# An eight-stage hybrid network on one core: a joint value and denominator product in local attention, two norms in a row as one, input and result moved tile by tile

## The reference

```
def _layernorm(x, axis=-1, eps=1e-05):
    m = jnp.mean(x, axis=axis, keepdims=True)
    v = jnp.var(x, axis=axis, keepdims=True)
    return (x - m) / jnp.sqrt(v + eps)
def rms(x, w):
    return x * jax.lax.rsqrt(jnp.mean(x * x, axis=-1, keepdims=True) + EPS) * w
x = x + _L0_attn_a_ref(_layernorm(x, axis=-1), ...)
x = x + _L0_attn_b_ref(_layernorm(x, axis=-1), ...)
attn = jax.nn.softmax(sim, axis=-1)
out = jnp.einsum('bhwij,bhwjd->bhwid', attn, bv)
```

## Time and profile before

| | us |
|---|---|
| median of 3 runs | 6118.09 |
| the profiled execution | 6125.03 |
| its span, first to last instruction | 6123.2 |
| TensorE busy (share of the span) | 5316.8 (87%) |
| VectorE busy | 3563.9 (58%) |
| ScalarE busy | 3332.0 (54%) |
| GpSimd busy | 2568.9 (42%) |
| mean granted TensorE clock | 0.946 |

### The profile page before, as it was taken

How to read it: one execution, slowest core, us unless ns; L and a number is a source line. 1 busy time by engine, 2 the same in 40 slices (tenths; PEclk the granted TensorE clock), 3 DMA queues, 4 the chain that set the end, 5 groups by cost and what they waited for, 6 DMA issues and landing times. The chain is left out here.

```text
span 6123.2 us, 113557 instructions
## 1 busy us (share of the span) xinstructions
PE 5316.8 (87%) x39222; PEld 2810.7 (46%) x39222; DVE 3563.9 (58%) x4189; ACT 3332.0 (54%) x4968; POOL 2568.9 (42%) x1902
## 2 busy tenths in 40 slices
PE   5866888888888998999897999899897999787999
PEld 2322555555544554554343554555343444343443
DVE  4757999999964553554354554554554343554444
ACT  4745888888854553554454554455354333443343
POOL 1333999999943662663133662664231000000000
PEclk8986999999999999999898999999899999888999
DMA  1002111111110110110000110111000210001111
GB/s 43 17 10 83 31 31 32 32 30 31 31 52 24 43 43 10 42 42 19 4 15 25 42 42 14 42 41 28 28 15 20 55 41 14 0 0 28 38 33 28
DMA packets 143957, 182.98 MB, mean 30 GB/s; under 512 B 33584, under 2 KB 86960, under 8 KB 142512
## 3 DMA queue, kind: packets, MB, share of 16 engines
q1 hardware_dynamic: 143792, 180.85, 11.1%
HBM read 80.31 MB, written 12.85 MB: 15 GB/s over the span
## 5 line engine op out<-in xcount | busy, mean ns | idle before, releaser
L2502 POOL TENSOR_TENSOR arena<-arena,wbig 128x1024 f32<-128x1024 f32 x512 | 1191.4, 2472 | 107.7 <-ACT arena L2438 107.6
L2489 DVE TENSOR_TENSOR_SCAN arena<-banks,arena 128x1024 f32<-128x1024 f32 x512 | 1140.6, 2278 | 68.4 <-ACT banks L2433 49.4
L963 ACT ACTIVATE arena<-banks,wbig 128x512 f32<-128x512 f32 x512 | 351.8, 687 | 591.2 <-PE banks L921 582.5
L1020 DVE TENSOR_TENSOR arena<-arena 128x512 f32<-128x512 f32 x512 | 353.2, 692 | 470.7 <-ACT arena L963 436.4
L2433 ACT ACTIVATE banks<-banks 128x1020 f32<-128x1020 f32 x512 | 518.1, 1012 | 108.5 <-PE banks L2354 100.9
L1510 POOL TENSOR_TENSOR arena<-arena 128x512 f32<-128x512 f32 x256 | 354.9, 1386 | 527.3 <-DMA arena<-arena 527.3
L635 DVE TENSOR_REDUCE arena<-banks 128x4 f32<-128x1024 f32 (+1 forms) x384 | 401.7, 1046 | 280.0 <-PE banks L462 225.7
L2438 ACT COPY arena<-banks 128x1024 f32<-128x1024 f32 x512 | 520.8, 1017 | 51.2 <-POOL arena L2502 29.9
L571 ACT ACTIVATE Y<-banks 128x2048 f32<-128x2048 f32 x192 | 305.6, 1592 | 306.4 <-PE banks L498 236.4
L931 PE MATMUL banks<-arena,wbig 128*128 128x512 f32 x1024 | 463.5, 598 | 0.0
L921 PE MATMUL banks<-Z,wbig 128*128 x1024 | 459.1, 593 | 0.0
(11 more groups left out here) (304 smaller groups left out, 9887.0 us busy)
## 6 DMA issues: line engine op xcount, KB each, us to landing
arena<-arena SPq DMA_DIRECT2D x1024, 64.0 KB, 2.0
arena<-scratch_g SPq DMA_DIRECT2D x64, 512.0 KB, 10.8
wbig<-wbig SPq DMA_DIRECT2D x48, 240.0 KB, 3.1
wbig<-scratch_d SPq DMA_DIRECT2D x512, 16.0 KB, 1.7
wbig<-scratch_b SPq DMA_DIRECT2D x64, 128.0 KB, 2.2
wbig<-scratch_c SPq DMA_DIRECT2D x64, 128.0 KB, 2.1
arena<-Z SPq DMA_DIRECT2D x64, 128.0 KB, 2.1
wbig<-in_l_ffn SPq DMA_DIRECT2D x1, 4197.0 KB, 12.4
```

The source lines that it names most:

```text
L963: act.activation(hid[e % 2][:, f, :], hbank[f], ACT.Relu, bias=b1[:, e, f:f + 1])\
L1020: last = dve.tensor_tensor(hid[e % 2][:, f, :], hid[e % 2][:, f, :], gate[u][:, e, :], ALU.mult)
L2489: dve.tensor_tensor_scan(own, line(decay_bank[n % 2]), own, 0.0, ALU.mult, ALU.add)\
L2502: pool.tensor_tensor(four(h[par][:, m * 1024:m * 1024 + 1024]), four(us[n % 2]), Bs[par].unsqueeze(1).to_broadcast([128, 4, SEQ]), ALU.mult)\
```

## The change

It has five parts.

1. In `values` the ones move into the weights: v is laid out as [v of head 2f, ones, v of head 2f+1], 64 columns each, and each product takes 128 of these columns, so that one full-width product gives the values of a head in one half of the partitions and its denominators in the other. 16 passes on half the columns become 8 passes on all 128.
2. So the copy of v (L1349) writes with gaps, the Ln of the denominators (L1355) becomes two instructions of 64 partitions that read one half and write the other, the product L1452 becomes two of 64 partitions, and the first block fills the ones with two memsets of 128x512.
3. Two norms in a row are one. With centred x and variance v the second root is of (1+e2) v + e1 e2. `attn_b` has one norm with that root. In `l0_attn_a` one centred norm gives both results, with a second Ln and Exp on ACT and two products on DVE for each tile.
4. The constants are loaded first, then X in 8 DMAs of 256 KB each with its own semaphore; SP waits in that block for the constants alone. The first weights are issued after it. PE waits for its tile at each centring of the first norm.
5. The last norm issues a store on SP for each tile when it is done, in place of the one store after it.

The core of the diff:

```diff
@@ -120,17 +120,21 @@
...
-def copy_dram_stage(k, name, pairs):
+def load_stage(k, x, pairs):
...
     landed = [Count(k, f"landed{n}", 16) for n in range(len(pairs))]
+    tiles = [Count(k, f"x_landed{t}", 16) for t in range(TILES)]
     with k.nc.Block() as block:
...
                 sp.dma_start(dst, src).then_inc(landed[n].sem, 16)
+            for t in range(TILES):
+                cols = slice(t * TILE, (t + 1) * TILE)
+                sp.dma_start(k.X[:, cols], x[:, cols]).then_inc(tiles[t].sem, 16)
             for n in range(len(pairs)):
                 sp.wait_ge(landed[n].sem, landed[n].at(16))
-
+    return tiles
@@ -155,7 +160,8 @@
...
         pe_order += [("var", t)] + ([("center", t + ahead)] if center and t + ahead < TILES else [])
-        act_order += [("ln", t), ("exp", t)] + ([("sq", t + ahead)] if t + ahead < TILES else [])
+        act_order += [("ln", t), ("exp", t)] + ([("ln2", t), ("exp2", t)] if second is not None else [])
+        act_order += [("sq", t + ahead)] if t + ahead < TILES else []
     biased = any(b is not None for _, _, b in outs)
@@ -164,6 +170,8 @@
...
     pre = [k.arena.take(TILE) for _ in range(bufs)]
+    rs2 = [k.arena.take(TILE) for _ in range(bufs)] if second is not None else rs
+    root_last, look_last = ("exp2", "ln2") if second is not None else ("exp", "ln")
     cbank = [k.psum[:, u, :] for u in range(bufs)]
@@ -176,6 +184,8 @@
...
                 if what == "center":
+                    if landed is not None:
+                        pe.wait_ge(landed[t].sem, landed[t].at(16))
                     if t >= bufs:
@@ -183,7 +193,7 @@
...
                     if t >= bufs:
-                        pe.wait_ge(act_s.sem, act_s.at(0, f"ln{t - bufs}"))
+                        pe.wait_ge(act_s.sem, act_s.at(0, f"{look_last}{t - bufs}"))
                     pe.matmul(vbank[t % bufs], k.c["mean"], sq[t % bufs], start=True, stop=True)\
@@ -203,7 +213,14 @@
...
                         act.wait_ge(dve_s.sem, dve_s.at(0, f"z{t - bufs}"))
-                    act.activation(rs[t % bufs], vbank[t % bufs], ACT.Ln, bias=k.c[eps]).then_inc(act_s.sem, 1)
+                    act.activation(rs[t % bufs], vbank[t % bufs], ACT.Ln, bias=k.c[eps], scale=scale)\
+                        .then_inc(act_s.sem, 1)
+                elif what == "ln2":
+                    act.activation(rs2[t % bufs], vbank[t % bufs], ACT.Ln, bias=k.c[second[0]], scale=second[1])\
+                        .then_inc(act_s.sem, 1)
+                elif what == "exp2":
+                    act.wait_ge(act_s.sem, act_s.at(0, f"ln2{t}"))
+                    act.activation(rs2[t % bufs], rs2[t % bufs], ACT.Exp, scale=-0.5).then_inc(act_s.sem, 1)
                 else:
@@ -212,16 +229,17 @@
...
             for t in tiles:
-                dve.wait_ge(act_s.sem, act_s.at(0, f"exp{t}"))
+                dve.wait_ge(act_s.sem, act_s.at(0, f"{root_last}{t}"))
                 if biased and t >= bufs:
                     dve.wait_ge(dve_s.sem, dve_s.at(0, f"b{t - bufs}"))
-                for dst, w, b in outs:
+                for n, (dst, w, b) in enumerate(outs):
+                    root = rs2[t % bufs] if n else rs[t % bufs]
                     to = pre[t % bufs] if b is not None else columns(dst, t)
...
                     if w is None:
-                        last = dve.tensor_tensor(to, c, rs[t % bufs], ALU.mult)
+                        last = dve.tensor_tensor(to, c, root, ALU.mult)
                     else:
-                        last = dve.scalar_tensor_tensor(out=to, in0=c, scalar=w, in1=rs[t % bufs],
+                        last = dve.scalar_tensor_tensor(out=to, in0=c, scalar=w, in1=root,
                                                         op0=ALU.mult, op1=ALU.mult)
@@ -233,6 +251,16 @@
...
                     last.then_inc(dve_s.sem, 1)
+
+        if store is not None:
+            stored = Count(k, "stored", 16 * TILES)
+
+            @block.sync
+            def _(sp):
+                for t in tiles:
+                    sp.wait_ge(dve_s.sem, dve_s.at(0, f"b{t}"))
+                    sp.dma_start(columns(store, t), columns(outs[0][0], t)).then_inc(stored.sem, 16)
+                sp.wait_ge(stored.sem, stored.at(16 * TILES))
@@ -1044,11 +1072,12 @@
...
-def l1_ffn(k, name, w):
+def l1_ffn(k, name, w, store=None):
     norm_stage(k, f"{name}_ln", k.X, [(k.Z, None, None)], True, "eps5")
...
     mixture_stage(k, f"{name}_mix", k.Z, w, k.Y, k.H)
-    norm_stage(k, f"{name}_last", k.H, [(k.X, w["gamma"], w["beta"])], True, "eps5", add_to=k.X)
+    norm_stage(k, f"{name}_last", k.H, [(k.X, w["gamma"], w["beta"])], True, "eps5", add_to=k.X,
+               store=store)
@@ -1110,7 +1139,7 @@
...
     qkb = pairs(k.arena.take_bf16(8 * SEQ), 8)
-    v = [take(2 * 512).rearrange("p (c h d) -> p c h d", c=2, h=WHEADS) for _ in range(2)]
+    v = [take(2 * 4 * 192).rearrange("p (c f s d) -> p c f s d", c=2, f=4, s=3) for _ in range(2)]
     prob = [pairs(take(2 * 320), 2) for _ in range(2)]
@@ -1120,7 +1149,7 @@
...
     obank = [k.psum[:, 6 + n, :] for n in range(2)]
-    cleared = Count(k, "cleared", 5)
+    cleared = Count(k, "cleared", 7)
     ones = k.c["ones"]
@@ -1133,13 +1162,15 @@
...
             dve.memset(mx, 0.0).then_inc(cleared.sem, 1)
+            for par in range(2):
+                dve.memset(v[par][:, :, :, 1, :], 1.0).then_inc(cleared.sem, 1)
             for m, (scale, partner) in enumerate(((w["qs"], w["qp"]), (w["ks"], w["kp"]))):
...
                     .then_inc(cleared.sem, 1)
-            dve.wait_ge(cleared.sem, cleared.at(5))
+            dve.wait_ge(cleared.sem, cleared.at(7))
@@ -1235,12 +1266,10 @@
...
                     for r in range(2):
-                        pe.matmul(to[half_rows(r), first:first + n], v[par][:, c, 2 * f + r, :],
-                                  prob[f % 2][:, r, at:at + n], start=(c == 0), stop=True, skip_group_check=True)
-                for c, at, n, first in ((0, 0, 192, 0), (1, 192, 128, 128)):
-                    for r in range(2):
-                        last = pe.matmul(to[half_rows(r), SEQ + first:SEQ + first + n], ones[:, 0:WDIM],
-                                         prob[f % 2][:, r, at:at + n], start=False, stop=True, skip_group_check=True)
+                        last = pe.matmul(to[:, r * SEQ + first:r * SEQ + first + n],
+                                         v[par][:, c, f, r:r + 2, :].rearrange("p s d -> p (s d)"),
+                                         prob[f % 2][:, r, at:at + n], start=(c == 0 and r == 0), stop=True,
+                                         skip_group_check=True)
                 last.then_inc(pe_o.sem, 1)
@@ -1346,13 +1375,16 @@
...
                 for c in range(2):
-                    last = act.copy(v[par][:, c, :, :].rearrange("p h d -> p (h d)"), bank[c])
+                    last = act.copy(v[par][:, c, :, 0:3:2, :], bank[c].rearrange("p (f r d) -> p f r d", f=4, r=2))
                 last.then_inc(act_e.sem, 1)
...
                 act.wait_ge(dve_n.sem, dve_n.at(b, f"n{f - 2}") if f >= 2 else dve_n.before(b, f"n{f + 2}"))
-                act.activation(recip[f % 2], obank[f % 2][:, SEQ:2 * SEQ], ACT.Ln).then_inc(act_d.sem, 1)
+                for r in range(2):
+                    last = act.activation(recip[f % 2][half_rows(r), :], obank[f % 2][half_rows(1 - r), r * SEQ:(r + 1) * SEQ],
+                                          ACT.Ln)
+                last.then_inc(act_d.sem, 1)
                 act.wait_ge(act_d.sem, act_d.at(b, f"ln{f}"))
@@ -1449,7 +1481,10 @@
...
                     dve.wait_ge(pe_w.sem, pe_w.before(b, "wo"))
-                dve.tensor_tensor(oT[:, f, :], obank[f % 2][:, 0:SEQ], recip[f % 2], ALU.mult).then_inc(dve_n.sem, 1)
+                for r in range(2):
+                    last = dve.tensor_tensor(oT[half_rows(r), f, :], obank[f % 2][half_rows(r), r * SEQ:(r + 1) * SEQ],
+                                             recip[f % 2][half_rows(r), :], ALU.mult)
+                last.then_inc(dve_n.sem, 1)
@@ -2537,8 +2572,8 @@
...
 def l0_attn_a(k, name, w, weights):
-    norm_stage(k, f"{name}_ln", k.X, [(k.Z, None, None)], True, "eps5")
-    norm_stage(k, f"{name}_rms1", k.Z, [(k.H, w["norm_attn"], None)], False, "eps6")
+    norm_stage(k, f"{name}_ln", k.X, [(k.Z, None, None), (k.H, w["norm_attn"], None)], True, "eps5",
+               second=("eps5_eps6", 1.0 + 1e-6), landed=k.x_landed)
     softmax_attention(k, f"{name}_attn", k.H, w["wq"], w["wk"], w["wv"], False, k.X, qn=w["qn"], kn=w["kn"],
@@ -2644,13 +2679,13 @@
...
         k.scratch["g"] = nc.dram_tensor("scratch_g", (EXPERTS, TOKENS), F32).ap()
+        k.x_out = out
+        k.x_landed = load_stage(k, arrays["x"], [(cst[:, :], arrays["constants"]),
+                                                 (cstb[:, :], arrays["constants_bf16"])])
         weights = Weights(k, arrays, layouts, stages)
```

(8 more changed lines are left out.)

5 lines of the change are left out of this document (3 added, 2 removed).

## The result

The changed kernel takes 6130.0 us (median of 20 runs) beside 6118.9 us of the kernel before (20 runs): a ratio of 1.0016, 95% interval 1.001 to 1.0023. It is slower by 11 us, where 44 us less were forecast.

What follows compares the result with a forecast made beforehand. Local attention was taken as PE-bound, its trip set by a ring through row maxima, DVE's cosine and POOL. Attention -9.6, attn_b norms -20.4, opening -7.0, load -3.5, store -3.8 sum to -44.3: 6118.1 to 6073.8 us, range 6056 to 6092.

Steps and rivals of the forecast that it cites:

- a ring: Local attention: PE's work, row maxima of group 2, DVE's cosine and POOL's adds set the 25.1 us trip.
- 0.63 us of room, 0.45 once the trip is 0.18 shorter.: Ahead of POOL's first add: slack that was to hide ACT's second Ln, which delays its copy 0.13 to 0.24 us.
- The milder slower rival: Local attention: ACT's or DVE's added work costs 0.1 to 0.5 us a trip, giving 6091 to 6118; 8%.
- So the turn moves ... 0.18 us a trip.: PE, behind the value group on the ring: the turn starts at 2061.36, not 2061.54; 2.5 us a call.
- The ones of groups 0 and 1 stand ahead of the norm spreading on PE ... its 0.70 us at L1194 covers them.: DVE's added products, 0.38 us each, were to hide behind PE's 0.70 us wait for POOL.
- 2% for a granted clock that falls more often.: Whole kernel: chance left for the granted clock falling more often, with no time given; 2%.
- the product gains nothing: Rival: the turn stays where it was, attention pays the memsets alone, +3.2 us, giving 6086.6; 17%.
- ACT on the ring: Rival: the copy of v with gaps takes twice its time, 1.11 us in 60 trips, giving 6154; 3%.
- Memsets: Before the first trip of each local attention: the two memsets lie open and cost 0.8 us a call.
- Tail: End of each call: last trip and tail gain about 0.15 us on every group, 0.7 us in all.
- Opening and load: Start of kernel: joint opening norms bring -7.0 us, the earlier load -3.5 us.
- 25.1 or more: Sign of refutation: the local attention trip stays at this many us, where about 24.9 was forecast.

Runs made afterwards that it cites:

- n2: Changed kernel with Ln of denominators and DVE's product one instruction each, the division left out: 6086.9 us, ratio 0.9943.
- m1: Changed kernel with DVE's cosines of groups 2 and 3 ahead of the product of group 0: 6105.9 us, ratio 0.998.
- r1: q3 with ACT's reciprocal of the sequence before behind the first raw copy and both squares, DVE's product of it moved later too: 6107.0 us, ratio 0.9976.
- p2: m1 with PE's projection of group 0 ahead of the turn and ACT's raw copy ahead of its shift: 6100.9 us, ratio 0.9971.
- n3: n1 with the Ln of the denominators as two instructions of 64 partitions: 6114.1 us, ratio 0.9991.
- q4: p1 with ACT's copy of v ahead of the exponential of group 0: 6070.1 us, ratio 0.992.
- n1: Changed kernel with local attention as before, only norms, loads and store changed: 6086.5 us, ratio 0.9938.
- q3: p2 with ACT's copy of v ahead of the exponential of group 0: 6078.2 us, ratio 0.9934.
- n4: n1 with DVE's product of values and reciprocals as two instructions of 64 partitions: 6259.0 us, ratio 1.0214.
- p1: n1 with PE's projection of group 0 ahead of the turn and ACT's raw copy ahead of its shift: 6088.2 us, ratio 0.9946.

## Why the prediction was wrong

It failed in local attention, by 48 us: -9.6 were forecast, memsets included, and +38.3 came (33.8 in the calls, 4.5 around the memsets). 4.5 more came in the other stages, the norms behind it above all. The rest of the sum, -34.7, was right to 1 us. In the steady trip -0.18 us were forecast and +0.19 came: the passes alone give -0.05 (n2), ACT's second Ln takes these back (25.14 in m1), and DVE's second product adds 0.19 (the changed kernel less m1).

- **"So the trip's length is set by a ring: ... that add waits 0.62 us for DVE's cosine, the cosine stands on DVE behind the row maxima of group 2."** This is the step that failed. The 0.62 us are there whatever comes before: in the steady trips of all kernels but r1 POOL's first add starts 0.62 to 0.63 us after the end of its first sine, because the cosine that runs beside the sine ends 0.54 to 0.55 us after it, whether it started 0.2 us before the sine's end (p2) or 0.8 (n3). (In q4 it starts at 12.05 and the sine ends at 12.36, in n1 at 12.00 and 12.53, and the cosine ends at 12.90 and 13.08.) In r1 alone the cosine starts after the sine, and there DVE does set the add. The ring runs over ACT's copy of v, PE's projection, ACT's raw copy, the swap DMAs and POOL's first sine. The sine starts 4.50 to 4.53 us after the raw copy in the median trip of every kernel (4.7 in a few trips).
- **"0.63 us of room, 0.45 once the trip is 0.18 shorter."** There was none. n3 shows the price: a Ln of half the partitions delays the raw copy by 0.31 us and the trip by 0.31. In the changed kernel the second Ln cost less, about 0.05 us, since the product before it ends earlier. The milder slower rival, "0.1 to 0.5 us a trip", had the size of the steady trip, but was given 8%, since the room was taken for real, and its 6091 to 6118 doesn't reach 6130: the first trips, the tail and the other stages are in no term of the prediction.
- **"So the turn moves ... 0.18 us a trip."** The turn moved by 0.19, the trip by 0.05 (n2): the projection behind it waits for ACT's copy of v. Of the queue behind the turn the prediction had not asked what else it waits for. With that wait gone and the projection moved up, the joint kernel's trip goes from 25.07 to 24.7 to 24.8 (p2 to q3).
- **"The ones of groups 0 and 1 stand ahead of the norm spreading on PE ... its 0.70 us at L1194 covers them."** They stand ahead of two cosines that POOL needs, and of the add for which the norm spreading waits. This is the costliest of the failed steps. The term stood at nothing, and m1 shows what it was worth in the whole kernel: 24 of the 43.5 us that separate the changed kernel from n1, by medians from different chips, or about half. Part of it is clock.
- **"2% for a granted clock that falls more often."** It falls in the first two trips of a call, behind PE's longer waits: 125 us at the lower level for 76. These 2% named it, with no term and no time.
- **The rival "the product gains nothing" (6086.6)** met the time of n2 (6086.9) and n1 by chance: n1 has no joint product and no memsets, and n2, which has both, leaves ACT's and DVE's doubled work out, which the rival took as hidden. The rival "ACT on the ring" named the right engine and for its price a copy twice as long; the copy with gaps kept its length (1.07 us for two, as before).
- **Memsets**: 1.1 us a call for 0.8. **Tail**: forecast to gain 0.7 us a call with the last trip, it loses: the tail is 1.05 longer, since the two Ln and two products lie open there (n3 alone 1.06, n4 alone 0.43).
- **Norms of `attn_b`**: -20.4, as forecast. **Opening and load**: -8.9 for -10.5; the tile took 2.97 us for 3.00, but the small weights landed later (9.6 us from their issue) and the first norm started at 16.64 and not near 15. **Store**: -4.5 for -3.8; 256 KB land in 2.0 us in the median for 2.5.

Of the signs named, the eight passes, the missing 0.09 us, the two Ln, the one norm and the last DMA were seen. PE's wait at L1225 is 0.43 us in the steady trip, inside the 0.4 to 0.6 that were named, but by luck: PE's own work ends later there, it isn't that POOL ends earlier. The trip was "25.1 or more", which the prediction had called its refutation.

## What to carry to other kernels

A wait that follows another engine's end by the same distance in every trip isn't proof that this engine is late. Before a step is put on the ring, ask of each instruction behind it what else it waits for (here PSUM banks that another engine had not yet emptied), and treat room read off one idle row as a guess until an added delay shows it. A split into halves that is free on the engine that gains can cost a full instruction on each engine that reads the result; count those in front of the transfers first. And where a wait of PE grows, price the clock as well as the wait.

## What the runs showed of the hardware

- An instruction on half the partitions takes as long as one on all: Ln 0.38 us on 64x256 and on 128x256, DVE's product 0.42 to 0.43 on both.
- POOL and DVE hold each other up when both work on SBUF operands. A cosine takes 0.68 us alone, 0.73 (p2) to 1.32 (n3) beside the first sine, and up to 1.76 beside POOL's next operations; POOL's add takes 1.27 us alone and 1.5 to 1.8 beside DVE. The Trainium skill, SBUF — State Buffer, section SBUF: two separate sides, says that the two share a pair of ports by an exclusive lock, which the one that starts first keeps for its instruction, when DVE has two SBUF inputs. The trace agrees: the cosine ends 0.54 to 0.55 us after the sine, wherever it started beside it.
- In the 18 traces together PE waited 1.35 us or more ahead of the norm spreading in 64 trips. In 45 of them it then ran at the lower level for some 7 to 10 us, and the trip took 28.1 to 30.3 us; in the other 19 it kept the full clock, and the trip took 25.8 to 26.2. With waits of 0.95 us or less the clock fell behind the wait in 1 of 879 trips, the first two of each call left out.
- The product behind a group of half-array products starts 0.20 us after the group's last pass (5.02 to 5.23 in q4), behind the joint one 0.11 (4.88 to 4.99 in q3). The Trainium skill, TensorEngine Tiling (Array Packing), section Tiling Modes, says that a mode change drains the engine; the trace agrees, with 0.09 us at either end of the group, and behind it the next product's own first pass lasts 0.32 us to its second in q4, 0.22 in q3. Otherwise the two forms take nearly the same: from the first pass to the last 0.98 us for eight full-width passes and 1.03 for eight pairs.
- In the changed kernel and p1, where PE's queue waited for the copy of v until 5.26, the weight load of the first projection pass started with the pass, at 5.36, and the pass lasted 0.32 us to the next; in the kernel before, with the turn still under way, it started 0.11 us ahead of the pass, and 0.22 us lay between the passes. A wait in the queue isn't the only thing that does this: q4 has the same 0.32 with no wait, right behind the half-array group.
